# Channel stage with times as rows and four channels by 128 batches as columns, weights stationary

## What is computed

```python
x1 = x + _L0_attn_ref(_L0_cond_ref(x, itok_B_0_15, L0_cond_weights), ...)
y = irfft(rfft(x1 * mask, 1024) * rfft(kernel, 1024))[..., :512]
y = (y + x1 * mask * D[:, None]) * mask
w = (unpacked_6_bit - zero_point) * scale        # 512 x 512
out = x1 + einsum('bsk,nk->bsn', y, w) + bias
```

## Time and profile before

| | |
|---|---|
| median of 3 runs | 745.95 us (745.17 to 747.67) |
| profiled execution | 751.04 us, span 749.2 us |
| TensorE matmuls | 723.2 us, 97%, x7544 |
| VectorE | 613.0 us, 82%, x1107 |
| ScalarE | 391.0 us, 52%, x740 |
| GpSimd | 203.7 us, 27%, x201 |
| DMA, whole span | 51.52 MB, 69 GB/s |

### The profile page before, as it was taken

How to read it: one execution, slowest core, us unless ns; L and a number is a source line. 1 busy time by engine, 2 the same in 40 slices (tenths; PEclk the granted TensorE clock), 3 DMA queues, 4 the chain that set the end, 5 groups by cost and what they waited for, 6 DMA issues and landing times.

```text
span 749.2 us, 18126 instructions
## 1 busy us (share of the span) xinstructions
PE 723.2 (97%) x7544; PEld 597.5 (80%) x7544; DVE 613.0 (82%) x1107; ACT 391.0 (52%) x740; POOL 203.7 (27%) x201
## 2 busy tenths in 40 slices
PE   8899999999999999999999999999987899999996
PEld 6668687786978788787869787786766799999996
DVE  3699999998998777797767869777986688888887
ACT  4576565656566775746556565658553233332221
POOL 6300020020002010540300000000220887777772
PEclk9999999999999999999999999999998999999999
DMA  9600010010002001000200010021124178888861
GB/s 299 233 2 1 4 59 2 2 60 4 1 2 62 2 2 57 2 5 13 60 2 2 3 56 2 1 58 47 43 70 138 57 188 202 205 202 203 200 132 71
DMA packets 37073, 51.52 MB, mean 69 GB/s; under 512 B 7376, under 2 KB 23168, under 8 KB 36864
## 3 DMA queue, kind: packets, MB, share of 16 engines
q1 hardware_dynamic: 34848, 49.74, 24.6%
q0 software_dynamic: 1184, 0.56, 0.3%
q10 hardware_dynamic: 960, 0.06, 0.1%
HBM read 41.71 MB, written 8.63 MB: 67 GB/s over the span
## 4 chain that ended last, share of the span: by engine, by line
PE 84%; DVE 12%; ACT 2%; issue 2%; POOL 0%; DVEq 0%; ACTq 0%
PE ps L683 30%; PE ps L575 6%; PE ps L731 6%; PE ps L576 6%; PE ps L577 6%; PE ps L754 4%; PE ps L1010 4%; PE ps L1011 4%; PE ps L624 3%; PE ps L583 3%; PE ps L584 2%; PE ps L585 2%; PE ps L979 2%; DVE z_low L1383 1%; PE ps L967 1%
## 5 line engine op out<-in xcount | busy, mean ns | idle before, releaser
L1116 ACT ACTIVATE qt<-ps,m_bias 128x512 f32<-128x512 f32 x228 | 145.9, 685 | 91.6 <-PE ps L683 83.9
L683 PE MATMUL ps<-q_high,m_high 64*128 64x512 f32 x768 | 166.5, 399 | 1.2 <-DVE sc L1362 1.2
L683 PE MATMUL ps<-q_high,m_low 64*128 64x512 f32 x768 | 162.9, 389 | 0.7 <-issue 0.7
L683 PE MATMUL ps<-q_low,m_high 64*128 64x512 f32 x768 | 114.8, 388 | 0.0
L683 PEld LDWEIGHTS ps<-q_high,m_high 64*128 64x128 f32 x768 | 90.0, 185 | 16.5 <-issue 6.3
L683 PEld LDWEIGHTS ps<-q_high,m_low 64*128 64x128 f32 x768 | 90.5, 185 | 10.0 <-issue 1.1
L1383 DVE TENSOR_TENSOR z_low<-ps,z_high 128x512 fp32r<-128x512 f32 x128 | 79.7, 683 | 21.3 <-ACT z_high L1136 19.9
L683 PEld LDWEIGHTS ps<-q_low,m_high 64*128 64x128 f32 x768 | 82.2, 185 | 9.9
L1136 ACT CAST z_high<-ps 128x512 fp32r<-128x512 f32 x128 | 66.7, 597 | 21.0 <-PE ps L798 10.6
L502 POOL TENSOR_TENSOR o_sum<-o_part,o_part 128x512 f32<-128x512 f32 x7 | 9.1, 1302 | 230.3 <-ACT o_part L1146 230.3
L1305 ACT COPY x1T_far<-ps 128x128 f32<-128x128 f32 x32 | 8.5, 265 | 103.7 <-PE ps L979 103.7
(11 more groups left out here) (270 smaller groups left out, 1653.9 us busy)
## 6 DMA issues: line engine op xcount, KB each, us to landing
x_raw<-in_x_groups SPq DMA_DIRECT2D x32, 256.0 KB
x_s<-in_x SPq DMA_DIRECT2D x32, 256.0 KB, 5.3
out<-res SPq DMA_DIRECT2D x31, 256.0 KB, 3.4
toep_high<-taps_scratch SPq DMA_DIRECT2D x32, 192.0 KB, 4.2
toep_low<-taps_scratch SPq DMA_DIRECT2D x32, 192.0 KB, 4.8
w_raw<-in_w_groups SPq DMA_DIRECT2D x8, 512.0 KB, 7.5
toep_far<-taps_scratch SPq DMA_DIRECT2D x32, 64.0 KB, 5.2
rope_raw<-in_rope_rows SPq DMA_DIRECT2D x8, 192.0 KB, 6.7
```

The lines of the kernel that those rows point to most:

```text
L683: mm = pe.matmul(ps[:, fold_bank(u, j) + e, :], weights[rows, (GH * g + j) // 2, c, :], moving[c][rows, :], start=start, stop=stop)
L1116: act.activation(qt[:, j, :], ps[:, fold_bank(u, j) + j % 2, :], ACT.Identity, bias=m_bias[:, h:h + 1]).then_inc(s["qt_done"], 1)
```

## The change

Times become the rows of the channel stage and four channels by 128 batches its columns. The host lays out x, Wo, the words of the quantised weights and the vectors by (reversed) time, and turns the output back, so no transpose is left in the stage or ahead of it. A group is four channels. Attention products and the projection have weights (WoT, wfT) stationary and 512 columns moving; the convolution has Toeplitz blocks stationary. Scale, bias and bo become per-partition scalars. The zero point's rounding rest goes by the sum of y over all times: a reduction over the four blocks of 128 times on VectorE (`y_sum`), split high and low, then two products with a matrix of ones per group (`total`), then ScalarE's `rest_begun` and GpSimd's addition of x1 (`rest_ended`), and VectorE adds the projection. The whole zero point is subtracted by GpSimd when it makes wfT. The unpacking is one mask operation per block, with words repeated by the host; shift by the scale in ScalarE's copy. Masks move from VectorE to GpSimd. `turned`, `turned_ffn`, `turned_wo`, `ffn_high`, `projected_last` and x1T_far's copy are gone, with their waits; `wo_high()` follows `ffn_float(3)` in ScalarE's order of unit 14.

```diff
-    qw = t("qw", [P, TT, 3 * P], I32, at=wcT_at)
-    un = [t(f"un{n}", [P, P, 4], I32, at=wcT_at + (6 + 2 * n) * KB) for n in range(2)]
+    qw = t("qw", [P, TT, T], I32, at=wcT_at)
+    q_float = t("q_float", [P, TT, T], at=wcT_at)
...
+    wfT = t("wfT", [P, TT, T], F32R, at=m_at)
...
+    x_t = [t(f"x_t{n}", [P, TT, 4, B], at=at) for n, at in enumerate((m_at + 24 * KB, sc_at, qt_at, qt_at + 8 * KB))]
...
+    rest = [t(f"rest{n}", [P, 4, B], at=m_at + (36 + 2 * n) * KB) for n in range(RW)]
...
-            sp.dma_start(qw[:], d["L0_ffn_qweight"].rearrange("(t n) k -> n t k", n=P)).then_inc(s["ffn_in"], 16)
...
+            sp.dma_start(qw[:], d["ffn_words"]).then_inc(s["ffn_in"], 16)
             sp.dma_start(len_i[:], d["itok_B_8_3872"].partition_broadcast(P)).then_inc(s["len_in"], 16)
...
+            sp.dma_start(cols[:], d["columns"]).then_inc(s["cols_in"], 16)
+            sp.dma_start(z_row[:], d["zero_row"].partition_broadcast(P)).then_inc(s["row_in"], 16)
+            sp.dma_start(woT_raw[:], d["woT"]).then_inc(s["wo_in"], 16)
...
+            def store(i):
+                sp.wait_ge(s["res_done"], i + 1)
+                sp.dma_start(out[i // 4, :, i % 4], rest[i % RW][:]).then_inc(stored[i % RW], 16)
+
+            sp.wait_ge(s["t_ready"], GH * LAST)
+            load_x1(0)
+            sp.wait_ge(s["turn_done"], 4 * LAST)
+            load_x1(1)
+            sp.wait_ge(s["t_ready"], GH * NU)
+            sp.wait_ge(s["taps_stored"], 96)
             for c in range(R):
                 load_toep(c)
-                if c >= 4:
...
+            sp.wait_ge(s["s_ready"], 4 * NU)
+            load_x1(2)
+            load_x1(3)
+            for c in range(C + 6):
                 if c + R < C:
-                    load(c + R)
-            for n in range(2):
-                cols = slice(HALF * (1 - n), HALF * (2 - n))
...
+                    sp.wait_ge(s["conv_ready"], c + 1)
+                    load_toep(c + R)
+                if 0 <= c - 6:
+                    store(c - 6)
+                if c >= 8 and c % 4 == 0 and c // 4 + 2 < NG:
+                    sp.wait_ge(s["rest_ended"], c - 4)
+                    load_x1(c // 4 + 2)
...
+            pool.wait_ge(s["cols_in"], 16)
+            chain(pool.tensor_scalar(z_scale[:], z_c, 0.0, 63.0, ALU.max, ALU.min))
+            chain(pool.tensor_scalar(z_scale[:], z_scale[:], MAGIC, None, ALU.add))
+            chain(pool.tensor_scalar(z_scale[:], z_scale[:], MAGIC, None, ALU.subtract))
+            chain(pool.tensor_tensor(z_scale[:], z_scale[:], z_c, ALU.subtract))
+            pool.tensor_tensor(z_scale[:], z_scale[:], s_c, ALU.mult).then_inc(s["z_scaled"], 1)
+            pool.wait_ge(s["row_in"], 16)
+            chain(pool.tensor_scalar(z_row[:], z_row[:], 0.0, 63.0, ALU.max, ALU.min))
+            chain(pool.tensor_scalar(z_row[:], z_row[:], MAGIC, None, ALU.add))
+            chain(pool.tensor_scalar(z_row[:], z_row[:], MAGIC, None, ALU.subtract))
+            pool.wait_ge(s["len_in"], 16)
+            chain(pool.tensor_copy(len_f[:], len_i[:]))
+            for k in range(TT):
+                pool.tensor_scalar(mask[:, k, :], len_f[:], l_pos[:, 0:1], float(P * k), ALU.subtract,
+                                   ALU.is_gt).then_inc(s["mask_ready"], 1)
+                pool.wait_ge(s["mask_ready"], k + 1)
             pool.wait_ge(s["t_ready"], GH * LAST)
...
-            chain(pool.tensor_scalar(c_row[:], z_row[:], 0.0, 63.0, ALU.max, ALU.min))
...
-            pool.tensor_tensor(c_row[:], c_row[:], s_row[:], ALU.mult).then_inc(s["c_done"], 1)
+            for k in range(TT):
+                pool.wait_ge(s["wf_ready"], k + 1)
+                pool.tensor_tensor(wfT[:, k, :], q_float[:, k, :], z_row[:], ALU.subtract).then_inc(s["wfT_done"], 1)
+                pool.wait_ge(s["wfT_done"], k + 1)
...
+            for c in range(C + 5):
+                i = c - 5
+                if i >= 0:
+                    g, n = i // 4, i % 4
+                    pool.wait_ge(s["rest_begun"], i + 1)
+                    pool.tensor_tensor(rest[i % RW][:], rest[i % RW][:], x_t[g % RX][:, n], ALU.add).then_inc(s["rest_ended"], 1)
+                if c < C:
+                    g, ch = c // 4, c % 4
+                    pool.wait_ge(s["yh_done"], c + 1)
+                    if g >= 2 and ch == 0:
+                        pool.wait_ge(s["f_ready"], 4 * (g - 1))
+                    pool.tensor_tensor(y_low[g % 2][:, :, ch, :], y[c % 2][:], f(y_high[g % 2][:, :, ch, :]),
+                                       ALU.subtract).then_inc(s["yl_done"], 1)
...
+            def attention_out(g, tt):
+                i = 4 * g + tt
...
-            def turned(c):
...
-                    mm = pe.transpose(ps[:, 2 + q, t_ * P:(t_ + 1) * P], x1[q][:, t_ * P:(t_ + 1) * P], ident[:])
...
+                if i >= 2:
+                    pe.wait_ge(s["x1_done"], i - 1)
+                part = slice(tt * P, (tt + 1) * P)
+                three(ps[:, A_BANK[i % 2], :], woT_high[:, part], woT_low[:, part], run_of(o_high[g % 2][:]),
+                      run_of(o_low[g % 2][:])).then_inc(s["a_ready"], 1)
...
+                g, ch, q = c // 4, c % 4, c % 2
+                if ch == 0:
+                    pe.wait_ge(s["x1_low_done"], 4 * g + 4)
...
+                    three(ps[:, 4 + q, e * P:T].rearrange("p (t b) -> p t b", b=B), toep_high[c % R][:, rows],
+                          toep_low[c % R][:, rows], x1_high[g % 2][:, 0:TT - e, ch, :], x1_low[g % 2][:, 0:TT - e, ch, :],
+                          e == 0, False)
+                pe.matmul(ps[:, 4 + q, (TT - 1) * P:T], toep_far[c % R][:], x_t[g % RX][:, 0, ch, :], start=False,
+                          stop=True).then_inc(s["conv_ready"], 1)
...
+                pe.matmul(ps[:, TOTAL_BANK, :], ones_r[:], run_of(sum_high[:]), start=True, stop=False)
+                pe.matmul(ps[:, TOTAL_BANK, :], ones_r[:], run_of(sum_low[:]), start=False, stop=True).then_inc(s["total_ready"], 1)
...
+            def through_ffn(g, n):
+                i = 4 * g + n
+                if n == 0:
+                    pe.wait_ge(s["yl_done"], 4 * g + 4)
+                if i == 0:
+                    pe.wait_ge(s["wfT_done"], TT)
+                if i >= 3:
+                    pe.wait_ge(s["res_done"], i - 2)
...
-                    for part in (y_high[q], y_low[q]):
-                        first, last = k == 0 and part is y_high[q], k == TT - 1 and part is y_low[q]
-                        pe.matmul(ps[:, bank, 0:HALF], part[:, k, :], wfT_a[:, k, :], start=first, stop=last)
-                        mm = pe.matmul(ps[:, bank + 1, 0:HALF + 2], part[:, k, :], wfT_b[:, k, :], start=first, stop=last)
+                    left = wfT[:, k, n * P:(n + 1) * P]
+                    pe.matmul(ps[:, F_BANK[i % 3], :], left, run_of(y_high[g % 2][:, k]), start=(k == 0), stop=False)
+                    mm = pe.matmul(ps[:, F_BANK[i % 3], :], left, run_of(y_low[g % 2][:, k]), start=False, stop=(k == TT - 1))
...
+            for tt in range(TT):
+                attention_out(0, tt)
+            for c in range(C):
+                g, ch = c // 4, c % 4
+                if g + 1 < NG:
+                    attention_out(g + 1, ch)
+                if g >= 1 and ch == 1:
+                    total(g - 1)
+                convolved(c)
+                if g >= 1:
+                    through_ffn(g - 1, ch)
+            through_ffn(NG - 1, 0)
+            total(NG - 1)
+            for n in range(1, 4):
+                through_ffn(NG - 1, n)
...
                     values(0, 0, 0, 4)
                 values(u - 1, 1, 0, 4)
...
+            def x1_rounded(i):
+                g, tt = i // 4, i % 4
+                act.wait_ge(s["x1_done"], i + 1)
+                if g >= 2 and tt == 0:
+                    act.wait_ge(s["conv_ready"], 4 * (g - 1))
+                act.copy(x1_high[g % 2][:, tt], x_t[g % RX][:, tt]).then_inc(s["x1_high_done"], 1)
+
+            split(1)
+            for tt in range(TT):
+                x1_rounded(tt)
+            for c in range(C + 5):
+                g, ch, i = c // 4, c % 4, c - 5
+                if ch == 0 and 1 <= g <= NG:
+                    act.wait_ge(s["y_summed"], 4 * g)
+                    if g >= 2:
+                        act.wait_ge(s["total_ready"], g - 1)
+                    act.copy(sum_high[:], y_sum[:]).then_inc(s["sum_high_done"], 1)
+                if c + 4 < C:
+                    x1_rounded(c + 4)
+                if ch == 1 and 2 <= g + 2 < NG:
+                    split(g + 2)
+                if i >= 0:
+                    act.wait_ge(s["total_ready"], i // 4 + 1)
+                    act.wait_ge(s["z_scaled"], 1)
+                    if i >= RW:
+                        act.wait_ge(stored[i % RW], 16 * (i // RW))
+                    act.activation(run_of(rest[i % RW][:]), ps[:, TOTAL_BANK, :], ACT.Identity, bias=fb_c[:, i % 4:i % 4 + 1],
```

(66 more changed lines are left out.)

369 lines of the change are left out of this document (79 added, 290 removed).

## The result

The changed kernel takes 760.58 us (median of 4 runs, 758.92 to 760.76) where the kernel before takes 745.83 (4 runs beside it); the ratio is 1.0187, with a 95% interval of 1.0171 to 1.0202. I had forecast 748.5 with a range of 742 to 758: slower was right, the size was not, and the time lies outside the range.

The account below looks back on a forecast made before the run. A channel was taken to last as long as TensorE's matmuls, 4.86 us. Against the profiled run, +12.4 +1.1 −2 −8.8 = +2.7; with that run's 5.1 above the median 745.95 carried over, 748.5 us, range 742 to 758.

Parts of the forecast that it names:

- The strided sum: Channel stage, VectorE's sum over four blocks with a 512-byte step: taken at 0.62 us, upper end 1.24.
- rival 1 (a): Channel stage: a strided sum of 1.24 makes VectorE's loop 5.19, +18 us; at 0.93, +9. Rival 1 as a whole: 28%.
- Rival 1: Channel stage: VectorE becomes the pace, by a dear sum or waits with GpSimd; 753 to 767 us, chance 28%.
- The head of the stage and the projection: Channel stage's start: first convolution 6.9 us after it begins, first projection starting at 22.7; whole stage 156.4, giving 8.8.
- The end of the attention: Before the channel stage: GpSimd's longer queue delays VectorE's first scores 12.4 us, TensorE idles 14, slow clock adds 1.1.
- The instruction block: TensorE's 4.32 us idle up to 568.03, put down to late instructions: fewer instructions ahead should gain 2 us.
- rival 2: End of the attention: the instruction block arrives before TensorE needs it, idle time and slow clock go; 742.5 us, chance 17%.
- The transposes: End of the attention: 16 transposes of the projection's weights leave TensorE, 1.7 us less.
- rival 1 (b): Channel stage: VectorE subtractions wait for GpSimd; both splits losing 0.6 makes the stage 8 us longer. Rival 1: 28%.
- Transfers: Channel stage's loads and stores, 0.98 MB per channel at 218 GB/s: costed at nothing.

Follow-up runs that it names:

- the sum at 0.69: Changed kernel with the four-block sum reading 4 neighbouring elements instead of 4 elements 512 bytes apart: 756.16 us, ratio 1.0091 to the kernel before.
- the spread: Changed kernel, zero-point chain early, x1_rest and woT_low later, four Toeplitz loads and two x groups issued after the last output product: 736.12 us, ratio 0.9794.
- The second profiles: Both kernels profiled again without edits: kernel before 749.95 us, ratio 1.0002; changed kernel 764.84 us, ratio 1.0172.
- its order mended: Changed kernel, zero-point chain ahead of the last o_sum addition, x1_rest behind y, woT_low later: 743.97 us, ratio 0.9883; with loads delayed too, 736.12 us, 0.9794.
- its own loads spread: Kernel before with four Toeplitz tiles and two x tiles loaded only behind the last output product: 746.82 us, ratio 0.9954.
- the kernel with the short steps: Changed kernel reordered with delayed loads, the four-block sum replaced by an 8-byte-step reduction or copies of 128 elements at 4, 16 or 12 bytes: 731.85 us, one execution.

## Why the prediction was wrong, point by point

**The strided sum** is the term that failed. I put it at 0.62 "by that row", the unpacking with 12 and 16 bytes of step, with 1.24 as the other end, and it measures 1.10, some 1.02 from start to start: rival 1 (a), some two thirds of the way from 0.62 to its upper bound of 1.24. The row was the nearest in step but neither in shape nor in kind: it is a mask operation on 128 elements, and it reads at 12 bytes, which cost some 0.02 us in the copies here. VectorE's loop became 4.79 instead of 4.57 and stood above TensorE's 4.44 to 4.46; in 23 channels that is 6.2 of the 7.6 us by which the stage missed its 156.4. The rest is in the first four channels (first projection 23.7 after the stage's start, forecast 22.7) and the tail. Rival 1 gave +18 for a sum of 1.24 and +9 for 0.93; at 1.02 it would give some 12, and the stage lost 7.6, because my loop was 0.18 too long in its other parts (x1 with its wait 1.42 for 1.47, y 0.72 for 0.79, ScalarE's delay 0.06 for 0.11). The Trainium skill, "SBUF — State Buffer", Door 1, says in a note that consecutive accesses to one 16-byte line go at full speed if there are at least two of them, and that each access to a new line pays; the runs agree, 0.68 at 8 bytes and 1.07 at 16. I had read its "4 fp32" as free up to 16 bytes, which the runs contradict.

**The head of the stage and the projection.** The first convolution came 7.0 after the start (forecast 6.9). With the sum at 0.69 the stage took 156.0. Its order and its waits were right; that the total came within 0.4 is in part luck, since TensorE's channel was 4.44 to 4.46 for 4.48 and VectorE's other parts 0.18 shorter than counted.

**The end of the attention.** The chain was right in kind and in who waits. The addition of o_sum to the first scores: forecast 16.6 us, measured 17.7; the masks took 3.15 for 2.6 and the short steps on 128x4 1.8 for 1.2. TensorE's idle time was 15.05 for 14. The clock was at its lower level as forecast.

**The instruction block** was my one gain by guess, −2, and it did not come: 4.55 us in place of 4.32. With fewer instructions ahead, the wait came at a later place in TensorE's order (among the mask products, not at the first output product), but it was as long; the DMA load is what matters, as the spread shows, and the changed kernel has as much of it. That instructions are what comes late is still an inference, but a narrow one: from idle time that nothing releases, and from the packets of q8 that end 1.2 to 1.6 us ahead of its end each time. That is rival 2 turned down. The Trainium skill, "Runtime: NRT & Kernel Launch", Instruction fetch mechanics, has the fetch mostly hidden; if this reading holds, the runs here show it not hidden, 4.4 us, where the DMA engines are at 0.96 to 1.04, and hidden in the changed kernel where they are at 0.14.

**The transposes** gave 1.4 us up to the last addition (405.0 from the first to the last, 406.4 before), forecast 1.7. The second profiles have 404.5 and 406.1, which gives 1.6: the forecast fits within what repeats.

**VectorE and GpSimd waiting for each other**, rival 1 (b): in the changed kernel the low parts take 0.69 us in the mean over 19 channels; no loop is lost to it. It did not occur, as the order had suggested.

**Transfers**: nothing. The share was 0.83 to 0.91 and TensorE waited for none in the steady stage.

In sum, behind the head: +12.8 instead of +2.7. The 10.1 between are 7.6 of the stage, 2.2 between o_sum and the stage (1.1 of a longer chain, 2.0 of the gain that did not come, less 0.9 that I can't place), and 0.3 of the transposes. The other 1.9 of the 14.75 between the medians lie outside this stretch or in runs without a profile; the head, in which profiles of both kernels differ by up to 5 us, is the likely place, but that isn't shown. My chances had 28% on VectorE's pace and 50% on a forecast that held the row with the lower price; the two bounds were 0.62 and 1.24, and the range should have reached what the upper one gives.

## What to carry to other kernels

Price an access pattern by a row with the same operation, the same step and the same length, and if there is none, let the range hold the upper bound: a VectorE that is level with TensorE turns each 0.1 us of it into the pace. When steps move into the queue of an engine, ask what stands behind them and whether their data was there earlier; here the same instructions cost 13.6 us behind one addition and nothing ahead of it. And where TensorE idles with no releaser, look at the DMA share at that time: the two kernels had the same 4 us there, for which neither the old nor the new arithmetic was to blame. The changed kernel with its order mended takes 736.1 us, 2.1% below the kernel before in the same rounds; without the spread loads it is 1.2% below. Against the kernel before with its own loads spread (0.9954) some 1.6% are left, an estimate from two ratios of different rounds.

## What the runs showed of the hardware

**Steps.** In a VectorE reduction the cost of a strided read is all or nothing at the steps tried: none at 8 bytes, 0.4 us in 512 elements at 16, 32, 64 and 128 bytes and at 512. A copy of 128 elements pays some 0.02 us at 12 bytes and 0.04 at 16.

**A copy waits for GpSimd.** A copy of 128 elements takes 0.22 us, and 1.30 to 1.37 when it starts while a GpSimd subtraction or addition is running (12 of the 24 copies; one that starts 0.12 us ahead of an addition takes 0.27). VectorE and GpSimd in the kernel with the short steps:
```profile
655.37 1.32 DVE L1641 COPY y_sum<-y 128x128 f32<-128x128 f32 x1
```
```profile
655.25 1.35 POOL L549 TENSOR_TENSOR rest<-rest,x_t 128x512 f32<-128x512 f32 x1 [2.12 <-ACT rest L1258]
```
It ends 0.09 us after GpSimd's addition. The earlier trace rows showed this for two inputs; a copy has one. The reduction in the same kernel took 0.68 in all eight channels, also where it began inside one of GpSimd's additions (650.65, within 650.34 to 651.88). The Trainium skill, "SBUF — State Buffer", Who interferes with whom, has it so: a copy can take the port pair that VectorE shares with GpSimd, a reduction never does.

**Executions differ in their head.** GpSimd's first addition began between 129.3 and 135.1 us in the profiles of all these kernels, with the same work ahead of it but for the steps on the row number. A single time of either kernel can lie some 5 us from another for that alone; a landmark behind the head takes it out, and runs of both kernels in the same rounds make it smaller.
